# Self-attention's softmax sums inverted by logarithm, exponential and a Newton step

## The reference, cut to what matters

```python
def _layernorm(x, axis=-1, eps=1e-05):
    m = jnp.mean(x, axis=axis, keepdims=True)
    v = jnp.var(x, axis=axis, keepdims=True)
    return (x - m) / jnp.sqrt(v + eps)
...
        scores = jnp.einsum('bqhd,bkhd->bhqk', q, k) * SCALE
        weights = jax.nn.softmax(scores, axis=-1)
        out = jnp.einsum('bhqk,bkhd->bqhd', weights, v)
        out = out.reshape(B, T, NUM_HEADS * HEAD_DIM)
        return out @ Wo
...
    x = _layernorm(x + _L0_attn_ref(x, L0_attn_Wq, L0_attn_Wk, L0_attn_Wv, L0_attn_Wo), axis=-1)
```

## Time and profile before

| | us |
|---|---|
| median of three runs | 2270.21 |
| the profiled execution | 2274.56 |
| its span | 2272.4 |
| TensorE busy (matmul) | 2228.8 (98%) |
| VectorE busy | 1893.1 (83%) |
| ScalarE busy | 1860.4 (82%) |
| GpSimd busy | 1901.7 (84%) |

### The profile page before, as it was taken

How to read it: one execution, slowest core, us unless ns; L and a number is a source line. 1 busy time by engine, 2 the same in 40 slices (tenths; PEclk the granted TensorE clock), 3 DMA queues, 4 the chain that set the end, 5 groups by cost and what they waited for, 6 DMA issues and landing times.

```text
span 2272.4 us, 62004 instructions
## 1 busy us (share of the span) xinstructions
PE 2228.8 (98%) x25966; PEld 1965.4 (86%) x25966; DVE 1893.1 (83%) x2111; ACT 1860.4 (82%) x2231; POOL 1901.7 (84%) x1157
## 2 busy tenths in 40 slices
PE   8999999999999999999999999999999999999898
PEld 4468998899989998999888998999889998988886
DVE  6877888888888888888888888888888888888877
ACT  5357888888888888888888888888888888888855
POOL 8865988889888898889878897888888888899943
PEclk9999999999999999999999999999999999999999
DMA  8410000000000000000000000000000000010321
GB/s 238 125 47 12 9 9 18 6 11 8 16 9 9 11 9 16 9 9 11 16 9 9 9 18 6 11 9 9 16 9 11 9 9 9 9 39 22 96 80 33
DMA packets 65302, 57.80 MB, mean 25 GB/s; under 512 B 32768, under 2 KB 57856, under 8 KB 65024
## 3 DMA queue, kind: packets, MB, share of 16 engines
q1 hardware_dynamic: 65024, 53.81, 8.5%
HBM read 30.99 MB, written 15.47 MB: 20 GB/s over the span
## 4 chain that ended last, share of the span: by engine, by line
PE 85%; POOL 7%; DVE 3%; DMA 2%; ACT 2%; issue 1%; SPq 0%; POOLq 0%; DVEq 0%; ACTq 0%
PE psum L464 35%; PE psum L496 12%; PE psum L489 12%; PE psum L492 6%; PE psum L494 6%; PE psum L629 4%; PE psum L619 4%; POOL e_lo L1729 3%; PE psum L770 2%; PE psum L636 1%; DVE run_max L1174 1%; PE psum L818 1%; DMA fold_t<-run_max 1%; POOL e_hi L1723 1%; PE psum L798 1%
## 5 line engine op out<-in xcount | busy, mean ns | idle before, releaser
L1729 POOL TENSOR_TENSOR e_lo<-ring,e_hi 128x1024 f16<-128x1024 f32 (+1 forms) x665 | 1387.5, 2101 | 187.0 <-ACT ring L941 157.8
L926 ACT ACTIVATE ring<-psum 128x1024 f32<-128x1024 f32 (+1 forms) x672 | 674.5, 1004 | 169.1 <-POOL e_lo L1729 98.6
L1194 DVE SCALAR_TENSOR_TENSOR ring<-ring,psum 128x1024 f32<-128x1024 f32 (+1 forms) x672 | 793.6, 1188 | 0.4 <-PE psum L736 0.4
L1174 DVE TENSOR_TENSOR run_max<-psum,run_max 128x1024 f16<-128x1024 f32 (+1 forms) x560 | 670.2, 1197 | 143.1 <-ACT ring L926 138.7
L464 PE MATMUL psum<-qx_hi,k_hi 128*128 128x256 f16 x2632 | 717.8, 273 | 9.7 <-DVE run_max L1174 9.6
L464 PE MATMUL psum<-qx_hi,k_lo 128*128 128x256 f16 x2632 | 717.4, 273 | 0.0
L464 PE MATMUL psum<-qx_lo,k_hi 128*128 128x256 f16 x2632 | 717.3, 273 | 0.0
L496 PE MATMUL psum<-v_main,e_lo 128*128 128x129 f16 x4032 | 703.9, 220 | 0.0
L941 ACT ACTIVATE ring<-ring 128x1024 f32<-128x1024 f32 (+1 forms) x672 | 697.1, 1038 | 0.6
L489 PE MATMUL psum<-v_main,e_hi 128*128 128x257 f16 x2016 | 550.4, 273 | 2.8 <-POOL e_lo L1729 2.8
L492 PE MATMUL psum<-v_main,e_hi 128*128 128x129 f16 x2016 | 443.5, 220 | 0.0
(11 more groups left out here) (205 smaller groups left out, 3063.9 us busy)
## 6 DMA issues: line engine op xcount, KB each, us to landing
o_scratch<-o_buf SPq DMA_DIRECT2D x56, 128.0 KB, 1.9
raw<-o_scratch SPq DMA_DIRECT2D x14, 512.0 KB, 4.6
stage<-in_ctxT SPq DMA_DIRECT2D x6, 500.0 KB, 4.4
stage<-in_ctxT SPq DMA_DIRECT2D x12, 250.0 KB, 5.4
w_scratch<-wall SPq DMA_DIRECT2D x1, 2304.0 KB, 10.3
wall<-w_scratch SPq DMA_DIRECT2D x6, 384.0 KB, 3.3
x<-in_xT SPq DMA_DIRECT2D x4, 448.0 KB, 6.5
res<-in_x SPq DMA_DIRECT2D x1, 1792.0 KB, 17.6
```

The source lines that it names most:

```text
L926: a.activation(ring[:, f % SLOTS, 0:n], pair(f)[:, 0:n], ACT.Copy).then_inc(s_kept, 1)
L1174: v.tensor_tensor(run_max[:, 0:n], pair(f)[:, 0:n], before, ALU.max).then_inc(s_max, 1)
L1194: v.scalar_tensor_tensor(slot, slot, LIFT, psum[:, 6, 0:QB].unsqueeze(1).broadcast_to([P, t, QB]), ALU.add, ALU.subtract).then_inc(s_sub, 1)
L1729: g.tensor_tensor(e_lo[f % NEL][:, 0:n], slot, e_hi[f % NEH][:, 0:n], ALU.subtract).then_inc(s_lo, 1)
```

## The change

The reciprocal of the 128x224 sums (L1298) goes. ScalarE takes the logarithm of the sums out of PSUM into `logs`, waits for itself, and writes exp(-log) into `rden`: two instructions of 128x224 in each turn, queued behind `exp_weights(b, 0)` and ahead of the roots and of `exp_weights(b, 1)`. The last batch's are behind the loop. VectorE waits for the second one and makes a Newton step in three instructions of 128x224: sums (PSUM) x rden into `logs`; (logs - 2) x rden into `logs`, both inputs in SBUF; and values (PSUM) x -1 x logs into attT. Before, it had two.

The first norm's roots: the square root becomes a logarithm and exp(-0.5 log), 4 columns each. `inverse` was one reciprocal and is now three instructions of 112x4 with a wait between each, all with two SBUF inputs. The sum of variance and epsilon (L1317) goes to a tile of its own. The table set `natural_log_exp_and_others` is loaded at the head of ScalarE's queue. The waits on `s_agg` count eight for each group where they counted six. The second and the third norm stay as they are.

```diff
+        var = at(RVAR, "var", [T, 2, NB], F32)
...
-        rden = at(RUN, "rden", [P, 2, T], F32)
+        rden, logs = [at(RUN + 896 * i, n, [P, 2, T], F32) for i, n in enumerate(("rden", "logs"))]
...
+                def inverse_sums(b):
+                    a.wait_ge(h_av, b + 1)
+                    if b:
+                        a.wait_ge(h_nrm, b)
+                    a.activation(logs[:, :, :], psum[:, 4, 2 * T:4 * T].rearrange("p (jj t) -> p jj t", jj=2),
+                                 ACT.Ln).then_inc(h_log, 1)
+                    a.wait_ge(h_log, b + 1)
+                    a.activation(rden[:, :, :], logs[:, :, :], ACT.Exp, scale=-1.0).then_inc(h_rec, 1)
...
-                    a.wait_ge(s_agg, 6 * i + 5)
-                    a.activation(of, of, ACT.Sqrt).then_inc(s_sq, 1)
+                    a.wait_ge(s_agg, 8 * i + 5)
+                    a.activation(root_logs, var[:, 0, 4 * i:4 * i + 4], ACT.Ln).then_inc(s_sq, 1)
+                    a.wait_ge(s_sq, 2 * i + 1)
+                    a.activation(of, root_logs, ACT.Exp, scale=-0.5).then_inc(s_sq, 1)
...
+                    a.preload_act_table_set("natural_log_exp_and_others")
...
                         exp_weights(b, 0)
+                        if b:
+                            inverse_sums(b - 1)
                         if b - 1 in STATS:
                             roots(STATS[b - 1])
...
-                    v.reciprocal(rden[:, :, :], out_t[1]).then_inc(h_rd, 1)
-                    v.wait_ge(h_rd, b + 1)
+                    v.wait_ge(h_rec, b + 1)
+                    v.tensor_tensor(logs[:, :, :], out_t[1], rden[:, :, :], ALU.mult).then_inc(h_rd, 1)
+                    v.wait_ge(h_rd, 2 * b + 1)
+                    v.scalar_tensor_tensor(logs[:, :, :], logs[:, :, :], 2.0, rden[:, :, :], ALU.subtract,
+                                           ALU.mult).then_inc(h_rd, 1)
+                    v.wait_ge(h_rd, 2 * b + 2)
                     if b:
                         v.wait_ge(h_wop, b)
-                    v.tensor_tensor(attT[:, :, :], out_t[0], rden[:, :, :], ALU.mult).then_inc(h_nrm, 1)
+                    v.scalar_tensor_tensor(attT[:, :, :], out_t[0], -1.0, logs[:, :, :], ALU.mult,
+                                           ALU.mult).then_inc(h_nrm, 1)
...
-                    v.wait_ge(s_sq, i + 1)
-                    v.reciprocal(of, of).then_inc(s_agg, 1)
-                    v.wait_ge(s_agg, 6 * i + 6)
+                    v.wait_ge(s_sq, 2 * i + 2)
+                    v.scalar_tensor_tensor(step, root, -0.5, root, ALU.mult, ALU.mult).then_inc(s_agg, 1)
+                    v.wait_ge(s_agg, 8 * i + 6)
+                    v.tensor_tensor(step, step, of, ALU.mult).then_inc(s_agg, 1)
+                    v.wait_ge(s_agg, 8 * i + 7)
+                    v.scalar_tensor_tensor(root, step, 1.5, root, ALU.add, ALU.mult).then_inc(s_agg, 1)
+                    v.wait_ge(s_agg, 8 * i + 8)
```

More of the change, by code:

```diff
@@ L106, in build @@
         assert SMALL + 1024 <= SBUF and QREG % 32 == 0
+        RVAR = SMALL + 640
         yT_hi = at(0, "yT_hi", [P, 2, NT], F16)
@@ L171, in build @@
         wo32 = [at(o, f"wo{i}", [P, D], F32) for i, o in enumerate((RING + 11 * 4096 + 3072, RING + 43392))]
-        rden = at(RUN, "rden", [P, 2, T], F32)
+        rden, logs = [at(RUN + 896 * i, n, [P, 2, T], F32) for i, n in enumerate(("rden", "logs"))]
+        h_log, h_rec = sem("h_log"), sem("h_rec")
         mx = [at(SMALL + 32 * r, f"mx{r}", [T, 2, 8], F16) for r in range(2)]
@@ L1004, in exp_weights @@
                                  ACT.Exp, scale=DH_S ** -0.5).then_inc(h_exp, 1)
-                def roots(i):
-                    of = rstd[:, 4 * i:4 * i + 4]
-                    a.wait_ge(s_agg, 6 * i + 5)
-                    a.activation(of, of, ACT.Sqrt).then_inc(s_sq, 1)
+                def inverse_sums(b):
[6 more added lines that the diff above has]
+                    a.activation(rden[:, :, :], logs[:, :, :], ACT.Exp, scale=-1.0).then_inc(h_rec, 1)
+                def roots(i):
+                    of, root_logs = rstd[:, 4 * i:4 * i + 4], var[:, 1, 4 * i:4 * i + 4]
+                    a.wait_ge(s_agg, 8 * i + 5)
+                    a.activation(root_logs, var[:, 0, 4 * i:4 * i + 4], ACT.Ln).then_inc(s_sq, 1)
+                    a.wait_ge(s_sq, 2 * i + 1)
+                    a.activation(of, root_logs, ACT.Exp, scale=-0.5).then_inc(s_sq, 1)
                 def norm_high(b):
@@ L1087, in _ @@
                 self_attention()
+                inverse_sums(NB - 1)
                 a.wait_ge(s_tsave, 32)
@@ L1314, in statistics @@
                         v.bn_aggr(meanvar[:, b, :], stats[:, b, :]).then_inc(s_agg, 1)
-                    v.wait_ge(s_agg, 6 * i + 4)
+                    v.wait_ge(s_agg, 8 * i + 4)
                     of = slice(4 * i, 4 * i + 4)
-                    v.tensor_scalar(rstd[:, of], meanvar[:, of, 1], LN_EPS, None, ALU.add).then_inc(s_agg, 1)
+                    v.tensor_scalar(var[:, 0, of], meanvar[:, of, 1], LN_EPS, None, ALU.add).then_inc(s_agg, 1)
                 def inverse(i):
-                    of = rstd[:, 4 * i:4 * i + 4]
-                    v.wait_ge(s_sq, i + 1)
-                    v.reciprocal(of, of).then_inc(s_agg, 1)
-                    v.wait_ge(s_agg, 6 * i + 6)
+                    root, of, step = [t[:, 4 * i:4 * i + 4] for t in (rstd, var[:, 0, :], var[:, 1, :])]
+                    v.wait_ge(s_sq, 2 * i + 2)
[5 more added lines that the diff above has]
+                    v.wait_ge(s_agg, 8 * i + 8)
                 def norm_low(b):
@@ L1683, in norms @@
                 def norms(i):
-                    g.wait_ge(s_agg, 6 * i + 6)
+                    g.wait_ge(s_agg, 8 * i + 8)
                     for b in range(4 * i, 4 * i + 4):
```

## The result

| | median, us | runs | lowest to highest |
|---|---|---|---|
| before | 2270.77 | 14 | 2268.97 to 2272.19 |
| after | 2276.22 | 14 | 2272.84 to 2287.01 |

The account below looks back on a forecast made before the run. TensorE, 85% of the chain, was taken to bound the kernel. Waits and roots summed to +9.4, the clock added -3.1 and +2.5: +8.8, or 2279.0 us against a median of 2270.21; range 2271.5 to 2286 (8 in 10).

Parts of the forecast that it names:

- Direction and mechanism: VectorE's added two-SBUF-input operations wait for the end of GpSimd's current instruction; slower, chance 0.78.
- Term: 0, and up to 1: Turns 1 to 8: waits of 1.2 to 1.4 us by turn 7 are absorbed before the weight sums.
- The 2.03 idle us before the weight sums: VectorE's idle time before the last weight sums, said to take up the lateness of turns 1 to 8.
- Turns 9 to 14, 1.8 + 6.8 + 1.1: Waits on GpSimd: 1.8 in three ordinary turns, 6.8 in root turns 9 and 11, 1.1 in turn 14.
- A root turn without waits, +0.3: Roots queued behind the sums' inversion: attT of batch 8 at 106.87 against 106.57 before, 0.3 us slower.
- a first projection after the roots not later than 106.6: Turn 9, after batch 8's roots: named as a sign that the prediction is wrong.
- The chain, +0.05 inside 0.18 of slack: From TensorE's sums to attT's end: 2.02 us against 1.98, inside TensorE's slack of 0.18.
- The clock, -3.1 + 2.5: TensorE's 1.2 GHz fall at 94.0 to 100.9 avoided, -3.1; one new fall in turns 9 to 11, +2.5.
- The last roots, -0.4: The table load at 157.93 goes; TensorE was idle only 0.41 us there, so -0.4.
- the forecast's case: Whole kernel: waits decide, with clock variants; 2275 to 2286 us, chance 0.72.
- the rival of half-sized waits (+2 to +4): Half the waits plus the clock gain, +2 to +4; chance 0.18 together with vanished waits (2270.8).
- The other rivals: Faster by the clock, 2265.7, chance 0.04; table loads each turn, 2311, 0.02; clock falling twice with whole-instruction waits, up to 2286.

Follow-up runs that it names:

- e1: Changed kernel with the sums' first Newton product written to PSUM, so the middle step has one SBUF input; 2271.71 against 2270.71 us, ratio 1.0004.
- e4: Changed kernel with the sums inverted by VectorE's reciprocal as before, only the roots by logarithm, exponential and Newton step; 2270.01 us, ratio 0.9998.
- e6: Changed kernel with the first Newton product in PSUM for batches 8 to 15 only, SBUF for 0 to 7; 2274.66 us, ratio 1.0020.
- before again: The kernel before, unchanged, one more profiled execution; 2270.50 us, span 2268.4.
- after again: The changed kernel, unchanged, one more profiled execution; 2274.66 us, span 2272.5.
- e5: Changed kernel with the first Newton product in PSUM for batches 0 to 7 only, SBUF from batch 8 on; 2272.86 us, ratio 1.0014.
- e3: Changed kernel with GpSimd's 4.06 us subtraction made in eight pieces of 256 columns; 2275.47 us, ratio 1.0023.
- e2: e1 plus the roots of groups 0 to 2 in PSUM, so each tiny step has at most one SBUF input; 2271.67 us, ratio 1.0003.
- e11: e4 with the roots of groups 0 to 2 in PSUM, so their tiny steps have one SBUF input each; 2268.56 us, ratio 0.9992.
- e7: e2 with ScalarE's roots put ahead of its inversion of the sums; 2268.02 us, ratio 0.9993.
- e8: e7 without the Newton step on the sums, attT being values times the exponential's result; 2267.36 us, ratio 0.9989.
- e12: e7 once more, on another chip; 2267.95 us, ratio 0.9991.

## Why the prediction was right, and where its working was not

**Direction and mechanism: right.** It said that the added operations with two SBUF inputs wait for the end of GpSimd's instruction and that this decides. e1 takes only that away and 4.5 of 5.5 us go with it. It also said what the rows would look like: steps ending 0.24 behind GpSimd's. The Trainium skill, "SBUF — State Buffer", section on the two separate sides, calls the pair an exclusive lock for a whole instruction; the trace agrees (87.67 + 4.06 against 88.03 + 3.95), and no run bears out sharing by bandwidth. One row was misread on the way: the 4-column L1317, taken as a case of two SBUF inputs, has only one (`tensor_scalar` on meanvar). It waited all the same, 0.46 us against 0.17 elsewhere, and in e1 the same operation took 1.01; a TENSOR_REDUCE with one SBUF input (89.07, above) ran at its usual 2.45 beside a 4.09 us instruction of GpSimd. So two inputs in SBUF are not the only case that waits. That 4-column steps with two inputs do wait, the later rows show (1.07 in after, 0.90 and 1.07 in e4).

**"Term: 0, and up to 1" for turns 1 to 8: wrong.** They carry 3.25 (e6 less e1). Three steps of it failed. The 2.03 idle us before the weight sums, taken as the cover, were read from one execution; before again has 0. And the waits themselves were put at 0.6, then 0.3 each, from GpSimd's rhythm, without the subtraction of 4.06. And the sum began with batch 2; in after again batch 1 has the longest wait of the ordinary turns there, 0.77 (a step of 1.16).

**Turns 9 to 14, 1.8 + 6.8 + 1.1: wrong in size.** They carry 1.45 (e5 less e1); e5's trace has 1.2 us of waiting in its eight steps. I took an operation issued at a chance time; the waits came to 0.15 on average, not 0.73, and they don't fall by chance: in after again, e3 and e5 the same three steps wait (batches 11, 12 and 13, each within 0.01 of 0.87, 0.61 and 0.81) and the other five take 0.39. In after, whose turns lie otherwise, it is other steps. The root turns were the worst: the prediction gave the third tiny step a fresh instruction of 1.4 and the normalisation another; e2 measures nothing for the tiny steps, and e4 with e11 perhaps 0.9 for all of them together.

**A root turn without waits, +0.3: about right.** The working had attT 2.67 us after the sums before and 2.97 after; turn 9 gives 2.67 and 3.05 in the two executions shown, +0.4. (As a sign of being wrong it named a first projection after the roots not later than 106.6. In after again it begins at 103.66, but in before again at 101.32: a clock time of one execution is no sign for another.) What it didn't ask is what the order costs against a turn without roots: 0.8, which e7 takes away.

**The chain, +0.05 inside 0.18 of slack: too small.** From TensorE's last sums to attT's end, turn 10:

```profile
105.52 1.56 DVE L1298 RECIPROCAL rden<-psum 128x224 f32<-128x224 f32 x1 [0.59 <-PE psum L591]
...
107.86 0.36 ACT L1014 ACTIVATE logs<-psum 128x224 f32<-128x224 f32 x1 [1.14 <-PE psum L595]
108.25 0.39 ACT L1017 ACTIVATE rden<-logs 128x224 f32<-128x224 f32 x1
108.77 0.39 DVE L1318 TENSOR_TENSOR logs<-psum,rden 128x224 f32<-128x224 f32 x1 [1.50 <-ACT rden L1017]
109.62 0.39 DVE L1325 SCALAR_TENSOR_TENSOR attT<-psum,logs 128x224 f32<-128x224 f32 x1
```

From the start of the first pass: 105.52 to 107.50, 1.98, against 107.86 to 110.01, 2.15. The two passes of ScalarE take 0.36 and 0.39, and VectorE starts 0.13 after the exponential's end, where the working had 0.02 to 0.03. So +0.17 uses up the slack; an ordinary turn in e1 takes 6.41 to 6.42 (attT's ends at 54.00, 60.42, 66.83) against 6.32 in before again (53.69, 60.01, 66.33), and in e8, where the chain is 0.8 shorter, 6.32 again. Some of it comes back where VectorE is late and its list is shorter: attT's distance between the two "again" executions falls from 2.68 (batch 5) to 1.54 (batch 7). That is read from them, not tested.

**The clock, -3.1 + 2.5: not a property of the kernel.** The fall at 94 us in before's profiled execution is absent in before again. Nor does it carry the median: the mean granted clock is 0.999 in eight of after's 14 executions, with a median of 2276.1, and where before has 0.999 beside the experiments its medians are 2270.7, 2270.3 and 2270.1. Long falls as in after's profiled execution (0.994) are in that one alone. In the two executions of after at 1.000 (2272.8 and 2273.1) the distance to before's at 1.000 (2269.3) is 3.7.

**The last roots, -0.4: too small by 0.2.** The distance between after again and before again shrinks from 5.40 at the last attT (153.52 against 148.12) to 4.8 at the scores above. It is the same everywhere: from the last attT to these scores it is 39.17 us in both executions of before and 38.57 in all twelve of the versions without the table loads, -0.6.

So two errors were large and opposite: +3.25 was left out in turns 1 to 8, and some 7 too much was charged to turns 9 to 14 (9.7, of which 0.9 was order, against 1.45). The result lies between the forecast's case and the rival of half-sized waits (+2 to +4), and the range held because it reached down to that; the likeliest value was 3.3 too high. That the sum came as near as this is luck: the two errors offset each other. The other rivals fell: no table loads, and after's lowest run (2272.84) is above the highest of before beside it (2272.19).

**What stays open:** how the executions differ in the times of their first loads, and so how the waits of one execution make the median; how often the step of batch 6 meets the 4.06 us subtraction; and by how much e7 beats before by what it computes. Its interval reaches 1.0002, and most of the difference is in the rest of the span. At equal clock some is left: the seven executions of e7 and the seven of e12 with a mean granted clock of 1.000 have medians of 2268.0 and 2267.5, before's beside them 2269.3 (two and four executions).

## What to carry to other kernels

- Before adding a VectorE operation with two SBUF inputs to a chain beside a busy GpSimd, give it one input in PSUM if a few columns are free there: same instruction, same 0.39 us, and the median fell by 4.5 us for 16 uses.
- When a table load is to be removed, look first whether it runs beside another engine's work; here it did, and what replaced it had to be put ahead of the waiting pass to be worth as much.
- Don't take idle time as cover on the word of one execution: 2.03 us became 0 in the next one of the same kernel. A long wait seen once (3.95) says as little: in the next execution it was not there.
- A small change of the total doesn't say that a saving did nothing. e8 was 4.86 us ahead near the end of the stage and lost 2.8 of it in a wait for another engine and a slower clock; look along the timeline for where a gain goes.

## What the runs showed of the hardware that was not expected

In all 14 kept executions TensorE waits 2.1 to 2.7 us for `run_max` once near 1190 us. In some the clock then falls to 1.2 GHz for about 3.4 us in the midst of dense work; in others it doesn't. Timeline of the matmul behind that wait, and the granted clock behind it, in before again and in e12:

```profile
1191.75 0.28 PE L464 MATMUL psum<-qx_hi,k_hi 128*128 128x256 f16 x1 [2.26 <-DVE run_max L1174]
1193.00:1195.00 2.00, 2.00 (x15) 1.69 (x14) 0.15 (x1) 1.21 (x2) 0.63 (x1) 0.50 0.00 0
...
1190.94 0.28 PE L468 MATMUL psum<-qx_hi,k_hi 128*128 128x256 f16 x1 [2.36 <-DVE run_max L1194]
1193.00:1195.00 2.00, 2.00 (x25) 1.84 (x23) 1.48 (x3) 2.00 (x3) 0.51 (x1) 1.00 0.00 0
```

The wait is as long in one as in the other (2.26 and 2.36). What differs is when it begins. In the thirteen executions shown beside before's first, it began before 1189.0 in e8, e12 and e7 and no fall followed; it began between 1189.49 (before again) and 1206.46 (after) in the other ten, and all have one. The first execution of before is the exception: its wait began at 1195.38, and the clock stayed at 2.4 GHz. Without the fall the rest of the span in the table above is 2078.9 to 2079.8, with it 2079.8 to 2081.3: in the middle some 1.5 us. So a gain of this size measured at the end is not all due to what was edited; e7 was half a microsecond ahead of before again at 187 us and 2.7 at the end. Why the moment should decide isn't settled; these executions only show that the two go together, but for one. The three without the fall are also the three with the roots put ahead of the inversion, so moment and version can't be told apart by them. These three do have a fall of the same length later, at 2134 to 2136 us (after, e3 and e5 have one like it, at 2141 to 2155 us, beside theirs near 1190), and their rest is the shortest all the same.
